# The way into the third mixer in stages, its convolution folded into the projection, and three counts for the expert tiles' loads

## The reference, cut to what matters

```python
# third mixer, on h = layernorm(x)
xz = jnp.einsum('btd,ed->bte', x, in_proj_w)            # 256 outputs
x_in, z = xz[..., :Dd], xz[..., Dd:]
x_conv = silu(conv1d(x_in, conv_w, padding 3 on the left, one filter of 4 per channel) + conv_b)
ssm_params = jnp.einsum('btd,ed->bte', x_conv, x_proj_w)   # B (16), C (16), one value for dt
dt = softplus(ssm_params[..., -1:] * dt_proj_w + dt_proj_b)
dA, dBx = exp(dt * A), dt * B_ssm * x_conv
h_t = dA_t * h_(t-1) + dBx_t                            # 16 states for each channel
y_t = sum over n of h_t[n] * C_t[n]
x = x + (y * silu(z)) @ out_proj_w.T

# second feed-forward part, for each of 16 experts on its 320 rows
expert_outputs = silu(rows @ w_gate) * (rows @ w_up) @ w_down
```

## Time and profile before

| | |
|---|---|
| median of 3 runs | 1153.38 us (1152.8 to 1153.68) |
| the profiled execution | 1153.68 us, span 1151.9 us |
| mean granted clock of PE | 0.953 |
| busy: PE, DVE, ACT, POOL | 88%, 55%, 47%, 17% of the span |
| expert tiles | 613 to 682 us |
| way in (first gather to first scan) | 690.65 to 750.93 us |
| scan loop to the last addition | 750.93 to 879.8 us |

### The profile page before, as it was taken

How to read it: one execution, slowest core, us unless ns; L and a number is a source line. 1 busy time by engine, 2 the same in 40 slices (tenths; PEclk the granted TensorE clock), 3 DMA queues, 4 the chain that set the end, 5 groups by cost and what they waited for, 6 DMA issues and landing times.

```text
span 1151.9 us, 11536 instructions
## 1 busy us (share of the span) xinstructions
PE 1012.3 (88%) x3673; PEld 439.1 (38%) x3700; DVE 629.3 (55%) x1175; ACT 538.7 (47%) x979; POOL 193.6 (17%) x173
## 2 busy tenths in 40 slices
PE   4799999998799999999769968677777999999896
PEld 2345544454222222233235643222223444444343
DVE  2222323334888868775253435589995554545564
ACT  3232232233367667676533434665664324464540
POOL 9100000000000000000574540076661000000000
PEclk9799999999899999999979988989999899999998
DMA  8620000030021202100003425000000211110032
GB/s 176 202 85 0 1 1 1 15 75 0 22 70 43 69 23 70 43 22 2 24 21 92 117 82 151 0 1 1 0 1 0 91 48 47 47 45 19 6 105 73
DMA packets 66588, 54.41 MB, mean 47 GB/s; under 512 B 18440, under 2 KB 58397, under 8 KB 66436
## 3 DMA queue, kind: packets, MB, share of 16 engines
q1 hardware_dynamic: 64228, 50.96, 15.7%
q0 software_dynamic: 2304, 2.76, 0.8%
HBM read 41.65 MB, written 13.77 MB: 48 GB/s over the span
## 4 chain that ended last, share of the span: by engine, by line
PE 68%; DVE 13%; ACT 8%; issue 7%; DMA 2%; POOL 1%; SPq 1%; another core or an unknown queue 1%; DVEq 0%; ACTq 0%; POOLq 0%
PE psum L675 65%; ACT sb_scr L1556 5%; DVE sb_scr L2201 3%; DVE sb_scr L2528 2%; DVE sb_scr L2537 2%; ACT psum L1556 1%; PE psum L832 1%; PE psum L1248 1%; DVE sb_scr L2076 0%; ACT sb_qstack L1556 0%; POOL expert_in L636 0%; DVE sb_x L2052 0%; DMA sb_scr<-pick_rows 0%; DVE sb_scr L2074 0%
## 5 line engine op out<-in xcount | busy, mean ns | idle before, releaser
L1556 ACT ACTIVATE sb_scr<-psum 128x512 f32<-128x512 f32 (+4 forms) x644 | 320.6, 537 | 369.0 <-PE psum L675 301.5
L675 PE MATMUL psum<-sb_h,sb_wide 128*128 128x512 f32 x448 | 210.6, 600 | 0.8 <-ACT sb_scr L1556 0.8
L2201 DVE TENSOR_REDUCE sb_scr<-psum 128x2 f32<-128x1024 f32 x128 | 154.8, 1222 | 46.4 <-PE psum L675 45.8
L675 PE MATMUL psum<-sb_scr,sb_wide 128*128 128x512 f32 x256 | 127.7, 600 | 0.3 <-DVE sb_scr L2578 0.3
L675 PEld LDWEIGHTS psum<-sb_h,sb_wide 128*128 128x128 f32 x448 | 83.7, 193 | 93.6 <-issue 91.9
L675 PE MATMUL psum<-sb_kstack,sb_qstack 96*128 96x512 bf16 x256 | 98.3, 395 | 11.3 <-DVE sb_scr L2201 8.5
L2140 DVE TENSOR_SCALAR sb_scr<-psum,sb_b 128x512 f32<-128x512 f32 x48 | 34.6, 747 | 126.3 <-PE psum L675 126.3
L658 POOL TENSOR_TENSOR sb_scr<-sb_scr 128x512 f32<-128x512 f32 x64 | 80.9, 1267 | 104.2 <-ACT sb_scr L1556 104.1
L1556 ACT ACTIVATE sb_scr<-psum,sb_b 128x512 f32<-128x512 f32 x48 | 31.2, 685 | 137.4 <-PE psum L675 137.4
L675 PE MATMUL psum<-sb_qstack,sb_kstack 128*128 128x512 bf16 x233 | 90.7, 395 | 4.4 <-ACT sb_scr L1556 3.2
L2568 DVE TENSOR_TENSOR sb_scr<-psum,sb_scr 128x512 f32<-128x512 f32 x64 | 44.1, 689 | 81.7 <-ACT sb_scr L1556 81.7
(11 more groups left out here) (255 smaller groups left out, 1306.2 us busy)
## 6 DMA issues: line engine op xcount, KB each, us to landing
sb_scr<-weight_rows SPq DMA_DIRECT2D x32, 256.0 KB
sb_qstack<-q_bounce SPq DMA_DIRECT2D x48, 96.0 KB
sb_kstack<-k_bounce SPq DMA_DIRECT2D x144, 32.0 KB
sb_scr<-pick_rows SPq DMA_DIRECT2D x8, 512.0 KB
expert_in<-sb_scr SPq DMA_DIRECT2D x4, 645.0 KB, 6.6
sb_scr<-expert_in SPq DMA_DIRECT2D x8, 322.5 KB
expert_out<-sb_scr SPq DMA_DIRECT2D x4, 512.0 KB, 4.9
sb_scr<-expert_out SPq DMA_DIRECT2D x8, 256.0 KB, 4.8
```

What stands on the lines that cost most here:

```text
L675: return nc.tensor.matmul(out_, w, r, start=start, stop=stop, **kw)
L1556: return nc.scalar.activation(out_, in_, func, **kw)
L2201: v.reduce_max(headmax[:, g % 2, t:t + 2, j], banks, AX.X).then_inc(sem("maxed"), 1)
```

## The change

1. **Convolution folded into the projection.** Once, ahead of the way in, `wconv[:, k]` is made as the x half of the projection's weights with each output channel scaled by its tap k: one matmul (ones times `conv_diag`, which spreads the taps) and one DVE multiplication. `convolve(b)` is then four matmuls on h with shifted columns, and the x projection, the copy into `xpad` and `xpad` itself go.
2. **Stages in place of batches.** ACT does all four squares and deviations, then loads the SiLU table once, does the four `conv_silu` and `gate_silu`, and goes back to the other table once. PE's and DVE's lists are written out by hand to fit.
3. **Softplus and dt by batch.** Only batch 0's are ahead of the scan loop. ACT does batch 1, 2 and 3's `softplus` after rounds 2, 5 and 8 of the loop, and DVE their `steps_taken` after rounds 5, 8 and 11. For this `dtv`, `dtl` and `xconv` move to other memory.
4. **Loads counted apart.** Rows, gate and up, and down weights of a pair each have a semaphore of their own. `gate_and_up` and `down` wait for theirs, `turn_in` for the rows alone. The weights of the first two pairs are issued after `stack_maxima(0, 0)` of the second mixer.

```diff
-            for q in range(2):
-                load_gate_up(q)
-                load_down(q)
             bounce(0)
             for g in range(GROUPS - 1):
                 stack(0, g)
             stack_maxima(0, 0)
+            for q in range(2):
+                load_gate_up(q)
+                load_down(q)
             stack_batch(0, True, False)
@@ PE, expert tiles
-                    pe.wait_ge(x_loaded[r], PAIR_LOADS * (u + 1))
+                    pe.wait_ge(x_loaded[r], 16 * (u + 1))
             def gate_and_up(u, c, n, begin):
+                if c % PT == 0:
+                    loaded, before_ = up_loaded[c // PT]
+                    pe.wait_ge(loaded, 32 * (u + 1) + before_)
@@ PE, way in
             def convolve(b):
-                pe.wait_ge(sem("xin_ready"), b + 1)
+                pe.wait_ge(ln_done, N2LN + b + 1)
                 if b >= 2:
                     pe.wait_ge(sem("xconv_ready"), b - 1)
-                for k in range(DCONV):
-                    m = mm(bank(4 + b % 2), conv_diag[:, k, :], xpad[:, b, k:k + S], k == 0, k == DCONV - 1)
+                for back in range(DCONV):
+                    m = mm(psum[:, 4 + b % 2, back:S], wconv[:, DCONV - 1 - back, :], h[:, b, 0:S - back], back == 0, back == DCONV - 1,
+                           skip_group_check=True)
@@ ACT, way in
+            for b in range(NB):
+                square(NB * ATTN2, b, 2)
+                deviation2(b)
+            nc.scalar.preload_act_table_set("silu_and_others")
+            for b in range(NB):
+                conv_silu(b)
+                gate_silu(b)
             nc.scalar.preload_act_table_set(LOG_EXP)
-            softplus(NB - 2)
-            act.wait_ge(sem("dtx_ready"), NB)
+            softplus(0)
@@ ACT, scan loop
                 decay_of(i)
                 if i + COPIES_AHEAD < NSCAN:
                     take_b(i + COPIES_AHEAD)
+                if i in (2, 5, 8):
+                    softplus(i // 3 + 1)
@@ DVE, way in
+            combine(0)
+            add_routed(0)
+            combine(1)
+            add_routed(1)
+            combine(2)
+            normalize2(0)
+            add_routed(2)
+            combine(3)
+            normalize2(1)
+            add_routed(3)
+            normalize2(2)
+            normalize2(3)
+            for b in range(NB):
+                state_inputs(b)
+            steps_taken(0)
@@ DVE, scan loop
+                if i in (5, 8, 11):
+                    steps_taken(i // 3)
```

More of the change, by code:

```diff
@@ L1267, in _ @@
             pe.wait_ge(sem("ffn1_loaded"), 16 * N_FFN1)
-            pe.wait_ge(setup, SETUP.index("xpad") + 1)
-            subtract_mean, variance = norm_steps(ATTN2, 2)
+            pe.wait_ge(setup, SETUP.index("conv_diag") + 1)
+            mm(bank(0), ones[:], conv_diag[:].rearrange("p k d -> p (k d)")).then_inc(sem("conv_spread"), 1)
+            N2LN = NB * ATTN2
             def turn_back(b):
@@ L1300, in state_inputs @@
                 pe.wait_ge(sem("xconv_ready"), b + 1)
-                mm(bank(2 + b % 2), wT[:, WSSM, :], xconv[:, b, :])
-                mm(bank(4 + b % 2), dt_rep[:], xconv[:, b, :]).then_inc(sem("ssm_done"), 1)
-            turn_back(0)
-            for b in range(NB + 1):
-                if b < NB:
-                    subtract_mean(b)
-                if b >= 1:
-                    project_in(b - 1)
-                    convolve(b - 1)
-                if b + 1 < NB:
-                    turn_back(b + 1)
-                if b < NB:
-                    if b >= 2:
-                        pe.wait_ge(sem("bc_parts"), b - 1)
-                    variance(b)
-                if b >= 1:
-                    state_inputs(b - 1)
+                if b == 0:
+                    pe.wait_ge(ln_done, N2LN + NB)
+                if b >= 2:
+                    pe.wait_ge(sem("bc_parts"), b - 1)
+                mm(bank(6 + b % 2), dt_rep[:], xconv[:, b, :])
+                mm(bank(b % 2), wT[:, WSSM, :], xconv[:, b, :]).then_inc(sem("ssm_done"), 1)
+            turn_back(0)
+            pe.wait_ge(setup, SETUP.index("wconv") + 1)
+            center2(0)
+            turn_back(1)
+            variance2(0)
+            center2(1)
+            project_z(0)
+            turn_back(2)
+            variance2(1)
+            convolve(0)
+            center2(2)
+            turn_back(3)
+            variance2(2)
+            project_z(1)
+            center2(3)
+            convolve(1)
+            variance2(3)
+            convolve(2)
+            project_z(2)
+            state_inputs(0)
+            convolve(3)
+            project_z(3)
+            for b in range(1, NB):
+                state_inputs(b)
             pe.wait_ge(sem("bc_parts"), NB)
+            pe.wait_ge(sem("zgate_ready"), NB)
             NSCAN = NB * NSTATE
@@ L1806, in conv_silu, with gate_silu, deviation2 @@
                 f(xconv[:, b, :], bank(4 + b % 2), ACT.Silu, bias=conv_b[:]).then_inc(sem("xconv_ready"), 1)
+            def gate_silu(b):
+                act.wait_ge(sem("z_done"), b + 1)
+                f(zgate[:, b, :], bank(2 + b % 2), ACT.Silu).then_inc(sem("zgate_ready"), 1)
+            def deviation2(b):
+                n = NB * ATTN2 + b + 1
+                act.wait_ge(sem("ln_var"), n)
+                f(rstd[:, b, :], bank(6 + b % 2), ACT.Ln, bias=eps[:]).then_inc(sem("ln_logged"), 1)
+                act.wait_ge(sem("ln_logged"), n)
+                f(rstd[:, b, :], rstd[:, b, :], ACT.Exp, scale=-0.5).then_inc(sem("ln_rstd"), 1)
@@ L1808, in softplus @@
             def softplus(b):
                 n = 3 * b
-                for i in range(2):
-                    act.wait_ge(sem("dtv_ready"), b + i + 1)
-                    f(dtl[:, b + i, :], dtv[:, b + i, :], ACT.Abs).then_inc(sem("dtl_step"), 1)
-                for i in range(2):
-                    act.wait_ge(sem("dtl_step"), n + i + 1)
-                    f(dtl[:, b + i, :], dtl[:, b + i, :], ACT.Exp, scale=-1.0).then_inc(sem("dtl_step"), 1)
-                for i in range(2):
-                    act.wait_ge(sem("dtl_step"), n + 2 + i + 1)
-                    f(dtl[:, b + i, :], dtl[:, b + i, :], ACT.Ln, bias=one[:]).then_inc(sem("dtl_step"), 1)
@@ L1821, in _ @@
[L1821 to L1833 removed]
+                act.wait_ge(sem("dtv_ready"), b + 1)
@@ new lines, in softplus @@
+                f(dtl[:, b, :], dtv[:, b, :], ACT.Abs).then_inc(sem("dtl_step"), 1)
+                act.wait_ge(sem("dtl_step"), n + 1)
+                f(dtl[:, b, :], dtl[:, b, :], ACT.Exp, scale=-1.0).then_inc(sem("dtl_step"), 1)
+                act.wait_ge(sem("dtl_step"), n + 2)
+                f(dtl[:, b, :], dtl[:, b, :], ACT.Ln, bias=one[:]).then_inc(sem("dtl_step"), 1)
+            for b in range(NB):
+                square(NB * ATTN2, b, 2)
+                deviation2(b)
+            nc.scalar.preload_act_table_set("silu_and_others")
```

98 lines of the change are left out of this document (47 added, 51 removed).

## The result

Over six runs each the changed kernel took 1159.78 us (1156.36 to 1162.4), the kernel before 1153.09 us (1148.38 to 1156.1): ratio 1.0057, 95% interval 1.0029 to 1.0085. It is slower, by more than the 0.2% that the prediction counts as no change. The profiled execution took 1160.08 us, span 1158.2 us.

A forecast was written before the change was run, and what follows sets the result against it. PE was taken to bound the expert tiles, DVE the scan loop, with PE near its bound in the way in. −0.8 − 5.2 + 1.7 + 6.0 + 2.0 = +3.7 on 1153.68 gave 1157.4 us, range 1153.0 to 1160.0.

The forecast's parts named there:

- main case: Whole kernel: slower, at 1157.4 us, own range 1155.9 to 1159.5, chance .60.
- Expert tiles: Expert tiles: PE no longer waits for the down weights, −0.8 us, bounds 0 and −1.6.
- Weights issued later: SP's DMA list: eight loads moved behind the second mixer's first stack cost 0, upper bound 4.0 us.
- Way in: Before the first scan: staging gives −5.2 us (−3.5 to −7), half clock at the third convolution +1.7 (0 to 3.4).
- Clock in the loop: Scan loop: PE idles some 2 us three times, giving three half-speed rounds, +2.0 us, bounds 0 and 4.
- Softplus and dt in the loop: Scan loop: work moved in from before it adds +6.0 us, bounds 0 and 9.7.
- so 1.3 each: Scan loop, DVE: two dt and dtx pairs took 745.89 to 748.42, so three cost 3.9 us.
- DVE waits for it: Scan loop, after round 2: `decay_of(3)` stands behind the first softplus on ACT while DVE waits, 1.9 us.
- The clock holds: Way in and loop: neither gap drops the clock, 1153.7 us, no change, chance .19.
- Every table load counts: Way in: seven fewer table loads, each on the path, shorten it by 9.0 us, to 1153.6; chance .04.
- The low clock lasts: Way in and loop: clock terms +3.4 and +4.0, no softplus hidden, put at 1160.8 us, chance .09.
- The loop absorbs it: Scan loop: moved softplus and dt hide in its gaps, it grows by nothing, 1149.4 us, chance .08.

The follow-up runs named there:

- e0_same: The kernel before with no edit, profiled again on the second chip: ratio .9993 to before.
- e1_counts: The kernel before with only part 4 of the change (loads counted apart, first weights issued later), second chip: ratio .9959 to before.
- the second run: The kernel before with only part 4 of the change, run once more on the fourth chip: ratio 1.0003 to before.
- e4_change: The changed kernel with no edit, run again on the third chip: ratio 1.0020 to before.
- e6_filler: The changed kernel with three extra matmuls, results unused, in PE's gap ahead of the third batch's convolution, third chip: ratio 1.0000 to before.
- e2_mixer: The changed kernel without part 4 (parts 1 to 3 alone), second chip: ratio 1.0021 to before.
- e3_softplus: The changed kernel with all four softplus ahead of the loop, dt and dtx staying in it, second chip: ratio 1.0001 to before.

## Why the prediction was right, and where its terms were not

The forecast was slower, 1157.4 us against 1153.68, +3.7. Measured are +6.4 in the profiled executions (1160.08 against 1153.68), +6.7 between the medians, and ratio 1.0020 (+2.3) on a third chip. The direction is right, and the median of 1159.78 lies in the range of 1153.0 to 1160.0, by .2 us. That much is luck: the main case alone went to 1159.5, and what carried the sum beyond it were tiles that grew by 3.0, which no term allowed for and which only the slower kind of chip shows. On the third chip, where the tiles don't grow, +2.3 is near the forecast from the other side. By stages, first chip (in brackets the others, each against `e0_same`, the only profile of before there):

| term | forecast | measured |
|---|---|---|
| expert tiles | −0.8 | +3.0 (−1.0 on the second chip) |
| way in, with its clock | −5.2 + 1.7 = −3.5 | −2.8 (−3.4 second, −3.3 third) |
| loop, with its clock | +6.0 + 2.0 = +8.0 | +8.7 (+8.5 second, +6.9 third) |
| the rest | 0 | −1.9 |

The rows add up to 7.0; ahead of the tiles .1 and between tiles and way in .6 went, which gives the 6.3 by which the spans differ. The way in with its clock and the loop with its clock are right within 1.1 us on every chip. Their inner terms are less so.

**Expert tiles.** PE's waits for the down weights, .8 us on the first chip, went there, and the tiles still grew. On the second chip, where there was no such wait to win, they shrank by 1.0, so that −0.8 against −1.0 is no confirmation of the step. On the slower kind of chip the tiles with the counts apart take 69.3, 69.9, 71.7 and 71.9 us (the last with some 2.3 of lower clock), those with the counts together 68.2 and 68.7. Whether the counts cost 1 us or more there, or the stretch scatters by as much, is not settled; no run isolates it, nor why the engines stand there for no visible reason. The surplus of `e1_counts` (4.7 us by its ratio) is not explained either: 1.0 of tiles, .5 of loop and 2.6 of the rest in its profile make 4.1, but the rest swings by 2 us in kernels of every sort, and the second run gave 1.0003.

**Weights issued later.** Forecast was 0, and so it is: in the change SP issues the eight loads from 302.01 us on and the batch's stack from 306.03 to 310.28, and PE's matmul of the earlier trace rows begins at 317.84 with no wait for a DMA.

**Way in.** The gap was the best of the terms: 3.4 us of PE idling ahead of the third convolution were forecast, and 3.53 are seen. Its price of +1.7 is right by luck. Forecast was a convolution that takes 3.4 us more, half of it hidden because DVE ends the stage; seen is one that takes 5.36 − 3.59 = 1.77 more, since the clock was back at 1.00 before its end, and none of it is hidden, since taking the gap away gave back 1.7. The stages' own gain, forecast at −5.2, is then −4.6 and −5.2 by the two chips. The first scan comes at 750.35, outside the 744.9 to 748.3 that was to show the prediction right and past the 749 that was to show more half clock than said. It isn't more half clock: the way in began 2.24 us later, behind the longer tiles, and took .7 us more than forecast.

**Clock in the loop.** It falls after standstills of 2.88 and 2.16 us, where the rows of before left 2 us undecided. The length of a standstill doesn't decide it alone: in `e4_change` the clock fell behind 2.18 us and held behind 2.46 and 2.16. The same loop takes 136.0 and 135.5 us where the clock is low for less of it (`e4_change`, `e6_filler`), and 137.7 and 137.6 where it is low for longer (the change, `e2_mixer`). The 1.6 to 2.2 us between them are the clock's, by all that the rows show; how much it costs in all isn't shown. Softplus was named as what makes PE stand. In fact it's the dt pairs as well: in `e3_softplus`, with no softplus in the loop, it falls again (its scans at 771.66 and 774.22 are 2.56 us apart, the half-speed round).

**Softplus and dt in the loop.** Here the sum came near and both terms in it were wrong, which is luck again. Three pairs of dt and dtx were put at 3 x 1.3 = 3.9, and took 2.37, 2.42 and 1.99 = 6.8 us (763.40 to 765.77, 771.61 to 774.03, 779.40 to 781.39). Softplus was put at 1.9 + .6 + .6 = 3.1, and taking it out of the loop gave .5 at most, less than the clock makes between two profiles of one kernel. The step that failed is "so 1.3 each": the rows were taken where POOL was idle, and in the loop POOL multiplies for two thirds of every round (12.82 of 20 us in the earlier trace rows). And the step "DVE waits for it" counted softplus as an addition, where taking it out gave back little.

**Rivals.** *The clock holds* fell with the rows at .50. *Every table load counts* asked for a way in shorter by 9.0; it is 2.8 to 3.4. *The low clock lasts* is near the measured time by its number (1160.8) but not by its terms: it asked for 3.4 of clock in the way in and a loop that grows by 11.0, and they are 1.8 and 8.7. *The loop absorbs it* asked for a loop that grows by under 2.0; it grew by 6.9 to 8.7, all of it in rounds 2 to 16, counted from 0, and from scan 16 to scan 63 every kernel here takes 91.96 to 92.00 us.
